# Row maxima one and a half quads ahead, and the first loads on two queues, in an attention and mixture-of-experts layer

## What is computed

```
qkv  = x @ w_qkv + b_qkv              # reshaped to 16 heads of 512 x 24 per batch: q, k, v of 8 each
attn = softmax(q @ k.T / sqrt(8))     # per head, 512 x 512
x    = layernorm(x + (attn @ v) @ w_out + b_out)
gates = sigmoid(x @ Wg); the best 2 of 8 experts, their gates normalized to 1
out  = shared expert + sum of the 2 routed experts (silu(x W1) * (x W3)) @ W2, divided by 3
x    = layernorm(x + out)
```

## Time and profile before

| | us |
|---|---|
| median of 3 runs | 738.19 |
| lowest, highest | 734.01, 744.85 |
| the profiled execution | 739.75 |
| its span, first to last instruction | 738.0 |
| TensorE busy in the span | 657.1 |
| VectorE busy | 551.3 |
| ScalarE busy | 426.0 |
| GpSimd busy | 268.9 |
| mean granted clock of TensorE | 0.964 of full |

### The profile page before, as it was taken

How to read it: one execution, slowest core, us unless ns; L and a number is a source line. 1 busy time by engine, 2 the same in 40 slices (tenths; PEclk the granted TensorE clock), 3 DMA queues, 4 the chain that set the end, 5 groups by cost and what they waited for, 6 DMA issues and landing times.

```text
span 738.0 us, 16592 instructions
## 1 busy us (share of the span) xinstructions
PE 657.1 (89%) x4593; PEld 315.6 (43%) x4594; DVE 551.3 (75%) x1272; ACT 426.0 (58%) x973; POOL 268.9 (36%) x402
## 2 busy tenths in 40 slices
PE   1899999999999999999999999997979898887880
PEld 1232333333333433433333343332568676666660
DVE  4967777879979969987996997974566566765763
ACT  1056677667766757666775666666342354454552
POOL 3124114213342244143434224306053265555553
PEclk9999999999999999999999999999899999999985
DMA  4366675543244233333233323302320333343322
GB/s 79 72 147 138 150 142 109 112 110 78 54 95 92 52 75 81 68 85 79 54 62 82 93 54 72 73 2 58 100 59 22 82 84 98 93 139 108 100 73 71
DMA packets 161854, 62.65 MB, mean 85 GB/s; under 512 B 110586, under 2 KB 155516, under 8 KB 161808
## 3 DMA queue, kind: packets, MB, share of 16 engines
q1 hardware_dynamic: 152960, 46.46, 29.0%
q0 software_dynamic: 5648, 13.26, 5.9%
q10 hardware_dynamic: 3200, 2.36, 1.0%
HBM read 38.04 MB, written 24.26 MB: 84 GB/s over the span
## 4 chain that ended last, share of the span: by engine, by line
PE 78%; ACT 5%; issue 5%; DVE 5%; DMA 2%; another core or an unknown queue 2%; POOL 1%; SPq 1%; ACTq 0%; DVEq 0%; POOLq 0%
PE pvp L1006 17%; PE scoreB L986 16%; PE scoreA L972 15%; PE scoreB L1520 5%; ACT prob L883 3%; PE pvp L1507 2%; PE scoreA L1497 2%; PE scoreA L1499 2%; PE scoreA L1498 2%; PE shared L525 2%; PE shared L514 2%; PE scoreB L1447 1%; DVE mx L916 1%; PE shared L544 1%
## 5 line engine op out<-in xcount | busy, mean ns | idle before, releaser
L916 DVE TENSOR_REDUCE mx<-scoreA 128x2 f32<-128x1024 f32 x256 | 306.3, 1220 | 77.0 <-PE scoreA L972 74.1
L883 ACT ACTIVATE prob<-scoreB 128x512 f32<-128x512 f32 x512 | 279.8, 600 | 128.0 <-PE scoreB L986 122.4
L972 PE MATMUL scoreA<-ks,qs 72*128 72x512 bf16 x512 | 205.7, 409 | 12.6 <-DMA ks<-parts_dram 10.2
L986 PE MATMUL scoreB<-qs,ks 74*128 74x512 bf16 x512 | 200.5, 394 | 15.3 <-ACT prob L883 11.9
L1006 PE MATMUL pvp<-prob,v 128*32 128x512 f32 x1024 | 141.4, 626 | 0.8 <-ACT pv_sb L875 0.8
L972 PEld LDWEIGHTS scoreA<-ks,qs 72*128 72x128 bf16 x512 | 51.0, 102 | 156.1 <-DVE mx L916 65.5
L986 PEld LDWEIGHTS scoreB<-qs,ks 74*128 74x128 bf16 x512 | 49.8, 98 | 110.6 <-ACT prob L883 85.3
L1166 POOL DMA_INDIRECT y_dram<-prob x72 | 70.6, 981 | 71.3 <-ACT prob L1397 43.3
L810 POOL CAST parts<-qk 128x256 bf16<-128x256 f32 x32 | 12.7, 396 | 227.9 <-ACT v_raw L563 208.6
L488 POOL DMA_INDIRECT slots_dram<-rows,slot_i x64 | 63.3, 990 | 31.7 <-issue 17.4
L1397 ACT ACTIVATE prob<-scoreB,prob 128x128 f32<-128x128 f32 x72 | 26.5, 368 | 38.4 <-PE scoreB L1520 26.1
(11 more groups left out here) (172 smaller groups left out, 880.4 us busy)
## 6 DMA issues: line engine op xcount, KB each, us to landing
qs<-parts_dram SPq DMA_DIRECT2D x96, 96.0 KB
parts_dram<-parts SPq DMA_DIRECT2D x32, 192.0 KB
slots_dram<-blank POOLq DMA_DIRECT2D x9, 520.0 KB
prob<-slots_dram SPq DMA_DIRECT2D x72, 65.0 KB
ks<-parts_dram SPq DMA_DIRECT2D x64, 64.0 KB
prob<-y_dram SPq DMA_DIRECT2D x8, 512.0 KB
ks<-parts_dram SPq DMA_DIRECT2D x32, 96.0 KB
xin<-in_L_attn_x SPq DMA_DIRECT2D x32, 64.0 KB, 2.0
```

Of the source, the lines that this page charges most:

```text
L883: act.activation(prob[:, i % 2, j, 2 * u + c, :], scoreB[:, c], ACT.Exp, scale=SCALE).then_inc(exp_done, 1)
L916: dve.tensor_reduce(mx[:, i % 2, at // 2, at % 2 * 2:at % 2 * 2 + 2], scoreA[:, at % 2], AX.X, ALU.max).then_inc(max_done, 1)
L972: ins = pe.matmul(scoreA[:, at % 2, c], qs[0:KR, st, j, qc * P:(qc + 1) * P], ks[0:KR, st, j, :], start=True, stop=True)
L986: pe.matmul(scoreB[:, c], ks[0:KM, i, j, kc * P:(kc + 1) * P], qs[0:KM, i, j, :], start=True, stop=True).then_inc(b_ready, 1)
```

## The change

Score A runs 12 steps ahead of score B instead of 16 (`LAG = 4` steps of a stage less): stage q does steps 4 to 7 of quad q + 1 in its steps 0 to 3, and steps 0 to 3 of quad q + 2 in its steps 4 to 7. The new `score_step` says which. The wait for the stack goes to the first score A matmul of its quad. mT moves from step 1 to step 4, xT from step 4 to step 1, and ScalarE issues the maxima's DMAs after its exponentials of step 5 instead of 3. The weight splits are spread otherwise. At the start, the five k loads of the first stack go to ScalarE's queue, behind all its work of stage -3, and the two `bq` loads go from SyncE's queue to the very start of ScalarE's.

```diff
-        if at == 1 and (inner or 0 <= s + 1 < self.quads):
-            kinds.append("mT")
+        if at == 1 and (inner or s + 4 < self.quads):
+            kinds.append("xT")
...
-        if at == 4 and (inner or s + 4 < self.quads):
-            kinds.append("xT")
+        if at == 4 and (inner or 0 <= s + 1 < self.quads):
+            kinds.append("mT")
...
+    LAG = 4
...
-        SPLITS = [(QUADS - 2, at) for at in (1, 3, 5, 7)] + [(QUADS - 1, at) for at in (1, 3, 5, 6, 7)]
+        SPLITS = [(QUADS - 2, at) for at in (5, 6, 7)] + [(QUADS - 1, at) for at in (1, 2, 3, 5, 6, 7)]
...
+        def score_step(b, i, at):
+
+            ahead, step = divmod(at + 2 * 8 - LAG, 8)
+            i += ahead
+            return (b + i // 4, i % 4, step) if has(b, i, 0) else None
...
+        def load_q_stack(eng, par, st):
+            for r in range(3):
+                eng.dma_start(qs[PR * r:PR * (r + 1), st],
+                              parts_dram[par, 0].rearrange("h i (d c) t -> (i d) h (c t)", d=HD)) \
+                   .then_inc(stack_loaded[par], 16)
+
+        def load_k_stack(eng, par, st):
+            for row, i0, i1 in K_ROWS:
+                eng.dma_start(ks[row:row + HD * (i1 - i0), st],
+                              parts_dram[par, 1, :, i0:i1].rearrange("h i (d c) t -> (i d) h (c t)", d=HD)) \
+                   .then_inc(stack_loaded[par], 16)
...
+                    load_q_stack(sp, par, st)
+                    if not isinstance(b, int) or n > 0:
+                        load_k_stack(sp, par, st)
...
         def attention_scalar(act):
+            bias = b_qkv.rearrange("(c k d) -> c k d", k=3, d=HD)
+            for k in range(2):
+                act.dma_start(bq[:, k:k + 1], bias[:, k, :].rearrange("c d -> d c"), allow_slow_non_contiguous=True) \
+                   .then_inc(bias_loaded, 16)
...
-                        if j == 1 and u == 1 and has(b, i, 1):
+                        if 2 * j + u == LAG + 1 and has(b, i, 1):
...
+                if isinstance(b, int) and q == -3:
+
+                    act.wait_ge(parts_stored, 16)
+                    act.wait_ge(ones_set, 1)
+                    load_k_stack(act, 0, 0)
...
-                    if has(b, i, 2):
-                        dve.wait_ge(a_ready, 8 * (q + 2) + at + 1)
-                        dve.tensor_reduce(mx[:, i % 2, at // 2, at % 2 * 2:at % 2 * 2 + 2], scoreA[:, at % 2], AX.X,
+                    ahead = score_step(b, i, at)
+                    if ahead:
+                        bb, ii, step = ahead
+                        j, half = step // 2, step % 2
+                        dve.wait_ge(a_ready, 8 * (4 * bb + ii) + step + 1)
+                        dve.tensor_reduce(mx[:, ii % 2, j, 2 * half:2 * half + 2], scoreA[:, step % 2], AX.X,
                                           ALU.max).then_inc(max_done, 1)
...
-                if has(b, i, 2):
-
-                    pe.wait_ge(stack_loaded[i % 2], 16 * STACK_DMAS * (2 * b + i // 2 + 2))
...
+                        if step == 0 and c == 0:
+
+                            pe.wait_ge(stack_loaded[st % 2], 16 * STACK_DMAS * (2 * bb + st // 2 + 1))
                         if c == 0:
-                            need(pe, max_done, 8 * (q + 2) + at - 1)
+                            need(pe, max_done, 8 * (4 * bb + st) + step - 1)
```

More of the change, by code:

```diff
@@ L706, in attention_sync @@
             load_x(-1, 1)
[L707 to L710, removed]
             bias_low = b_qkv.rearrange("(q l k d) -> l k q d", q=NCH, l=4, k=3)
@@ L961, in stage @@
                 q = 4 * b + i
-                if has(b, i, 2):
-                    pe.wait_ge(stack_loaded[i % 2], 16 * STACK_DMAS * (2 * b + i // 2 + 2))
                 def score_a(at, c):
-                    if has(b, i, 2):
-                        st, j, qc = (i + 2) % 4, at // 2, at % 2 * 2 + c
+                    ahead = score_step(b, i, at)
+                    if ahead:
+                        bb, st, step = ahead
+                        j, qc = step // 2, step % 2 * 2 + c
+                        if step == 0 and c == 0:
+                            pe.wait_ge(stack_loaded[st % 2], 16 * STACK_DMAS * (2 * bb + st // 2 + 1))
                         if c == 0:
-                            need(pe, max_done, 8 * (q + 2) + at - 1)
-                        ins = pe.matmul(scoreA[:, at % 2, c], qs[0:KR, st, j, qc * P:(qc + 1) * P],
+                            need(pe, max_done, 8 * (4 * bb + st) + step - 1)
+                        ins = pe.matmul(scoreA[:, step % 2, c], qs[0:KR, st, j, qc * P:(qc + 1) * P],
                                         ks[0:KR, st, j, :], start=True, stop=True)
```

## The result

| | before | after |
|---|---|---|
| median of 20 runs each, taken together | 737.46 us | 748.19 us |
| lowest, highest | 731.38, 745.33 | 741.18, 752.76 |
| profiled execution, its span | 739.75, 738.0 | 745.32, 743.6 |
| ratio of the times | | 1.0146, 95% interval 1.0117 to 1.0176 |

The change makes the kernel slower by 1.5%, about 11 us; I had forecast 737.2. Within 2% of no change, but outside my range and on the other side of it.

A forecast was written before the change was run, and what follows sets the result against it. The prediction took the attention loop to be bound by TensorE. Its terms, -5.9 + 0.7 + 2.8 + 1.2 + 0.5 - 0.3 = -1.0 us from the median 738.19, gave 737.2 us, range 730.0 to 743.5.

The forecast's parts named there:

- part (d): Less room for loads: maxima +0.5 us (bounds 0 and 4.9), stacks -0.3, x tile 0, at most 0.5.
- (c): mT at step 4, xT at step 1: waits in stages i = 3 (+2.8 us) and i = 0 (+1.2), elsewhere 0.
- Part (a): Start: four steps fewer before stage 0 and two queues bring stage 0 to 33.6 us from 39.47, -5.9 us.
- the 35.5 that I had named as wrong: Sign at the start: stage 0 later than 35.5 us would show the forecast wrong.
- R4: Start comes forward less, through the maxima load or shared DMA engines: two us less gained, 739.2 us; chance 0.10.
- Part (b): Stage 30: four score A steps fall into its first half and cost +0.7 us.
- its larger term (+2.8): Stages i = 3: the x1 transpose waits behind mT, 0.55 us, counted 0.45 inside the loop; bounds 0 and 3.6.
- The 1.2 us for the stages with i = 0: ScalarE's maxima issues end late behind routing operations; 0.2 us at TensorE in each of six stages, bounds 0 and 3.
- R1: ScalarE's hand-over of the maxima loads costs every stage, 10.9 us instead of 1.2: 746.9 us; chance 0.12.
- R2: The two waits of (c) are hidden, so 4.0 us go: 733.2 us; chance 0.18.
- R3: Clock falls at step 5 of each loop pass's fourth stage: more, 740.5 us; none, 732.3; chance 0.18.

The follow-up runs named there:

- e1: The changed kernel with x tiles of stages i = 1, 2, 3 loaded one stage earlier; 742.92 us, ratio 1.0088 to the kernel before.
- e3: The changed kernel with all loads of the first stack and the bias loads back on SyncE's queue; 747.21 us, ratio 1.0138 to the kernel before.
- e4: The changed kernel with expert weights loaded in stages 3 to 7 instead of 0 to 4; 749.07 us, ratio 1.0198 to the kernel before.
- e7: The changed kernel itself once more, in a later series; 703.85 us, ratio 1.0156 to the kernel before.
- e8: The same kernel as e3 once more, in the series of e7; 700.97 us, ratio 1.0145 to the kernel before.
- c1: The kernel before with the same earlier x tile loads as e1, as a control; 736.30 us, ratio 1.0005.
- e2: The kernel before with only the first stack's k loads and the bias loads moved to ScalarE's queue; 738.54 us, ratio 1.0028.
- e10: A new version: 12 steps ahead only in stages -2 to 0, 16 from stage 1, first loads on SyncE; 739.70 us, ratio 0.9977 to the kernel before.
- e11: The same kernel as e1 once more, in the series of e10; 749.22 us, ratio 1.0107 to the kernel before.
- e12: The changed kernel with the edits of e1 and e3 together, in the series of e10; 746.96 us, ratio 1.0054 to the kernel before.
- f2: The changed kernel with the edits of e1 and e3, plus unused matmuls filling TensorE before stage 0; 737.66 us, ratio 0.9983 to the kernel before.
- f1: The kernel before with unused matmuls added during the first stack wait and in 16 early score A steps; 733.78 us, ratio 0.9981.
- e6: As e3, but 14 steps ahead, mT at step 2, xT at 4, maxima loads after step 3; 715.11 us, ratio 1.0331 to the kernel before.
- e9: The kernel before itself once more, for a second profile in the series of e6; 690.93 us, a single run.

## Why the prediction was wrong

**The step that failed.** In part (d): "The x tile loses three steps: ... Just in time: 0, at most 0.5." I checked it in stage 3 alone, from one landing of 5.1 us (the trace has it; the earlier trace rows show its neighbours, 6.7 and 4.8). It was not stage 3 that decided but three other places: stage -2 (5.14 us, ahead of score A in TensorE's stream; at the first score B e1 wins only 0.4 us there, as the k loads come next), stage 5 (once, 3.91 us) and stage 9 (1.7 to 3.1 us, in all five traces with the change's order of steps and of loads: after, e3, e4, e7, e8). The trace of before had the warning for stage 9. Its x tile goes out at 170.07, and step 1, where the change puts xT, stands at 171.14:

```profile
170.07 0.38 SPq L703 DMA_DIRECT2D xin<-in_L_attn_x  x1
...
171.14 0.27 PE L521 MATMUL shared<-ident,mx 128*16 128x128 f32 x1
```

At 1.9 us to landing that is about 0.8 us too late, before SyncE falls behind any further; in after the tile went out 3.1 us later than before, at 173.13. With all first loads on SyncE, loading the tile earlier took the ratio from 1.0138 and 1.0145 to 1.0034 and 1.0054: 1.0%, 7 us. With the two queues in place it was 0.5% (1.0146 and 1.0156 to 1.0088 and 1.0107). In the kernel before, the same edit does nothing (c1). I had also listed xT only as work that changes place in (c), and not written down what each moved job waits for.

**Part (a), the start: -5.9 forecast, -3.1 at the first score B, 1.7 to 3.3 kept.** The first score B came at 36.35, past the 35.5 that I had named as wrong. Score A at 19.43 instead of 17.3 is the x tile (5.14 us) and, hidden behind it, the two queues, which cost 0.9 us instead of winning 0.8 (e2). The maxima load took 3.31 us where I allowed about 2. That is R4, with the right mechanism, priced at only two us. What no step of mine had: TensorE is at its lower level until 54 to 63 us in nearly every trace, whether stage 0 begins at 35 or 39, so a start won ahead of that can be partly given back: in after, 3.8 us at the mark of stage -1 are 1.7 at stage 1 (3.6 and 3.3 in the second pair). In e10 5.6 us became 0.8, but 2.9 of those went to the four steps put back into stage 0 and only 1.9 to the slow stretch.

**Part (b): +0.7.** The four steps took 498.95 to 506.23, 7.28 us against 6.81: +0.5. Right.

**Part (c): +4.0.** Right in the mechanism of its larger term (+2.8): the x1 transpose waits 0.47 us behind VectorE's second mT operation, as laid out from the earlier trace rows, at a cost of 0.69 in a bare stage and 0.28 where another wait covers it, so 2 to 4 us over the six stages. A loop pass without a long stage was 0.5 us longer in the first pair and 0.84 in the second; I had 0.65. The 1.2 us for the stages with i = 0 don't show in the second pair, where stages of kinds 0, 1 and 2 are longer by 0.14 at most from stage 12 on. So R1 (ScalarE's hand-over in every stage) is out, and R2 (the waits hidden) too.

**Part (d), maxima loads: +0.5.** Mis-sized: 3.2 us of TensorE's waits in after, 2.0 to 4.1 in the runs with the same order and the weights in their place, all by stage 5 and under the expert weights (e4: 1.1). Where the clock falls behind the wait of stage 3, that stage alone loses 3.5 to 4.4 us (e3, e8, e11, e12, f2), so my upper bound, 4.9 from waits alone, was nearer than my term. The small size of the load and its own queue did not protect it. The rule of the Trainium skill that I weighed ("DMA: Bandwidth & Descriptors", "Queues, rings and completion order": an engine takes turns between its queues) would have made this term 0. The runs speak against it as a forecast of time: 4 KB on ScalarE's queue landed after 3.31 and 5.79 us.

**R3, the granted clock.** I gave it 0.18 and looked for it at one place in the loop. It can multiply a wait elsewhere: 3.09 us of waiting in stage 9 became 9.2, 3.91 in stage 5 became 7.8; but 2.06 us in stage 9 of e7 stayed 1.9. The mean granted clock is 0.960 over the 20 runs of after (mean 747.2 us); for before it is 0.970 over the 19 runs beside e1 to e4 (735.7), 0.969 over the 35 beside c1 (737.7) and 0.967 over the 23 beside e10 (741.7). Time times what is missing gives 30 us for after and 22 to 25 for before, so some 5 to 8 of the 11 us were lost at the lower level. This is an estimate from means of different series, and it leaves out the start, where the clock is printed as 1.00. In the loop itself, in the series that have falls there, a long stage (17 us instead of 15.4) came in 5 of 25 passes with the old order of steps and in 20 of 40 with the new. Why the new order should fall more often is not shown.

**The sum, redone,** from the marks of the two traces of the changed kernel, up to stage 30. First pair: start -1.7, stages 2 to 8 +2.5, stage 9 +9.2, stages 10 to 28 +0.4 (with one long stage fewer than before), stages 29 and 30 +1.8, in all +12.2. Second pair: start -3.3, stages 2 to 8 +11.6 (7.8 in stage 5, 2.5 in stage 3), stage 9 +1.9, stages 10 to 28 +4.0, the last two +0.1, in all +14.3. The medians differ by 10.7 and 11.9. In each trace one late x tile is the largest term, and it isn't the same tile. My range was too narrow because each wait was priced at its own length, and because a step with a margin of 0.4 us where I looked (85.9 against 86.3) was counted as zero everywhere.

## What to carry to other kernels

When an operation moves earlier in an in-order stream, list what it waits for at its latest occurrence, not at a typical one, and everything that then stands behind it: here one 64 KB tile cost up to 9.2 us in a single stage. Move the load with its user, in the same edit; it cost nothing here and was worth 0.5 to 1%. Don't put a job whose result is read late directly ahead of another user of the same PSUM bank.

## What the runs showed that I had not expected

- Two queues made eight loads of one stack land later than one queue: last landing at 19.0 instead of 18.1 us, 4.64 us instead of 2.95 for the last.
- TensorE ran at 0.63 us a score matmul until 54 to 63 us in all traces but one (73.66 in e2, where this made the stage before the rise 21.36 us long instead of 15.4), also when it was kept busy from 18 us on (f1). The trace prints the clock as 1.00 there, except in f1, where it prints 0.50. A matmul's duration is the surer sign.
- In the series of e6 to e9 the kernel before took 692 us, in the others 735 to 743. The record gives that series the same chip number as e1 to e4, which had 735, so it isn't shown that the chip makes the difference. In the trace of e9 the wait at step 5 doesn't occur, and stage 11 takes 14.15 us instead of 15.34; but of the 48.8 us between the two spans of before only 12.3 lie ahead of the mark in stage 30, the rest behind it. The cause isn't known. The ratio of the changed kernel was 1.0156, close to the 1.0146 of the first result.
